# One wq product of each attention layer taken in three f32r passes instead of f32

## The reference

```python
for i in range(12):
    qkv = x @ Wqkv[i].T + bqkv[i]
    q, k, v = jnp.split(qkv, 3, axis=-1)     # 16 heads of 8 channels
    att = jnp.einsum('bhqd,bhkd->bhqk', q, k) * scale
    y = jnp.einsum('bhqk,bhkd->bhqd', att, v)
    x = y @ Wproj[i].T + bproj[i] + x
x = _layernorm(x0 + x)
x = _layernorm(x + ffn(x))
```

## Time and profile before

| | |
|---|---|
| median of 3 executions | 348.29 us (347.01 to 348.66) |
| the profiled execution | 348.11 us, of it 346.3 us span |
| mean granted TensorE clock | 0.995 of full speed |
| TensorE matmul busy | 321.3 us, 93% |
| VectorE busy | 234.9 us, 68% |
| ScalarE (ACT) busy | 184.1 us, 53% |
| GpSimd (POOL) busy | 98.4 us, 28% |

### The profile page before, as it was taken

The page is one execution under the profiler, slowest core; times in us unless marked ns, Lnnn a source line. Parts: engine busy times, 40 slices in busy tenths (PEclk is TensorE's granted clock), DMA queues, the critical chain, the costliest instruction groups (busy, mean ns, idle before and its releaser), DMA issues.

```text
span 346.3 us, 8406 instructions
## 1 busy us (share of the span) xinstructions
PE 321.3 (93%) x3349; PEld 291.2 (84%) x3349; DVE 234.9 (68%) x652; ACT 184.1 (53%) x421; POOL 98.4 (28%) x91
## 2 busy tenths in 40 slices
PE   7596989999999999999999999999999999999994
PEld 7485877979989798897989979799797988888883
DVE  1047888777577575766758767576675568998974
ACT  2142673846748376573855738567383045533350
POOL 2012342305032050410505014050235032654533
PEclk9899999999999999999999999999999999999999
DMA  8910100101001020010100101010000000111112
GB/s 233 403 54 2 60 3 2 59 2 61 2 2 59 3 61 3 2 59 2 61 1 21 41 2 59 2 61 4 2 2 1 2 4 0 30 30 47 46 33 61
DMA packets 10659, 13.65 MB, mean 39 GB/s; under 512 B 512, under 2 KB 8832, under 8 KB 10496
## 3 DMA queue, kind: packets, MB, share of 16 engines
q1 hardware_dynamic: 8224, 11.35, 10.2%
q10 hardware_dynamic: 2400, 1.80, 1.6%
HBM read 11.04 MB, written 2.10 MB: 38 GB/s over the span
## 4 chain that ended last, share of the span: by engine, by line
PE 75%; DVE 11%; DMA 5%; issue 4%; ACT 2%; POOL 1%; ACTq 1%; POOLq 0%; DVEq 0%
PE ps L922 13%; PE ps L963 12%; PE ps L853 12%; PE ps L805 6%; PE ps L803 6%; PE ps L804 6%; DMA xt<-x_tok 5%; PE ps L1042 3%; PE ps L862 3%; PE ps L908 3%; DVE s_rows L636 2%; PE ps L869 2%; DVE xt L738 2%; DVE mt L624 2%; PE ps L1031 1%
## 5 line engine op out<-in xcount | busy, mean ns | idle before, releaser
L371 POOL TENSOR_TENSOR step_lo<-step,step_hi 128x512 fp32r<-128x512 f32 x44 | 54.8, 1275 | 159.6 <-ACT step_hi L461 159.6
L803 PE MATMUL ps<-state_hi,step_hi 128*128 128x258 f32 x176 | 50.7, 288 | 0.0
L922 PE MATMUL ps<-s_rows,w 32*128 32x256 f32 x768 | 44.8, 380 | 5.5 <-DVE s_rows L636 5.5
L805 PE MATMUL ps<-state_hi,step_lo 128*128 128x258 f32 x176 | 49.8, 283 | 0.0
L804 PE MATMUL ps<-state_lo,step_hi 128*128 128x258 f32 x176 | 49.6, 282 | 0.0
L922 PEld LDWEIGHTS ps<-s_rows,w 32*128 32x128 f32 x768 | 40.4, 185 | 7.4 <-ACT s_rows L455 7.4
L963 PE MATMUL ps<-step,gram 128*128 128x128 f32 x352 | 44.7, 281 | 1.2 <-DVE gram L631 1.2
L461 ACT CAST step_hi<-step 128x512 fp32r<-128x512 f32 x44 | 27.0, 619 | 35.4 <-DVE step L641 35.4
L963 PEld LDWEIGHTS ps<-step,gram 128*128 128x128 f32 x352 | 41.0, 192 | 5.4 <-DVE step L641 3.3
L853 PE MATMUL ps<-w,gram 128*128 128x128 f32 x352 | 44.0, 278 | 0.0
L853 PEld LDWEIGHTS ps<-w,gram 128*128 128x128 f32 x352 | 41.1, 192 | 1.0
(11 more groups left out here) (121 smaller groups left out, 512.9 us busy)
## 6 DMA issues: line engine op xcount, KB each, us to landing
w<-weights SPq DMA_DIRECT2D x12, 496.5 KB, 3.5
xchan<-x_chan SPq DMA_DIRECT2D x1, 2048.0 KB, 14.7
out<-xchan SPq DMA_DIRECT2D x7, 256.0 KB, 2.3
xt<-x_tok ACTq DMA_DIRECT2D x4, 256.0 KB, 9.8
xt<-x_tok SPq DMA_DIRECT2D x4, 256.0 KB, 5.7
fw_int<-ffn_weights ACTq DMA_DIRECT2D x1, 576.0 KB, 16.8
out<-xchan SPq DMA_DIRECT2D x2, 128.0 KB, 1.9
cst<-consts ACTq DMA_DIRECT2D x1, 154.5 KB, 4.6
```

The lines of the kernel that those rows point to most:

```text
L371: nc.gpsimd.tensor_tensor(group(step_lo, g), group(step, g), group(step_hi_f, g), ALU.subtract).then_inc(step_lo_ready, 1)
L803: nc.tensor.matmul(dst, l_hi, r_hi, start=True, stop=False)
L805: return nc.tensor.matmul(dst, l_lo, r_hi, start=False, stop=True)
L922: last = nc.tensor.matmul(n_banks(h)[:, k, :], w[r, s, WQ + P * i:WQ + P * (i + 1)], s_rows[r, h, i, :], start=i == 0, stop=i == QUADS - 1)
```

## The change

n_stage(0) stays as it is. For n_stage(1), ACT writes the high part of s (`s_hi`, f32r, two operations of two blocks each) and VectorE the low part (`s_lo`, two operations); wq is split once a layer into `wq_hi` (ACT, at the head of its layer) and `wq_lo` (GpSimd, at the head of its layer). n_stage(1) is then three f32r products for each i. VectorE's sum `mbq` moves behind the first two `add_identity`. SP waits for the split of wq before it loads over the slot.

```diff
+        s_hi = sb("s_hi", [P, QUADS, 2 * P], F32R)
+        s_lo = sb("s_lo", [P, QUADS, 2 * P], F32R)
+        wq_hi = sb("wq_hi", [P, QUADS, P], F32R)
+        wq_lo = sb("wq_lo", [P, QUADS, P], F32R)
 # SP
                 sp.wait_ge(shift_ready, k + 1)
+                sp.wait_ge(wq_split, k + 1)
 # GpSimd, first in the layer
+                pool.wait_ge(wq_hi_set, at(1, 1))
+                nc.gpsimd.tensor_tensor(wq_lo[:, :, :].rearrange("p r c -> p (r c)"), w[:, s, WQ:WQ + QUADS * P],
+                                        wq_hi[:, :, :].rearrange("p r c -> p (r c)").bitcast(F32),
+                                        ALU.subtract).then_inc(wq_split, 1)
 # ACT, first in the layer
+                act.wait_ge(w_in[s], at(8, 16 - 8 * s))
+                if at(1, 0):
+                    act.wait_ge(n_done, at(2, 0))
+                nc.scalar.copy(wq_hi[:, :, :].rearrange("p r c -> p (r c)"), w[:, s, WQ:WQ + QUADS * P]).then_inc(wq_hi_set, 1)
 # ACT, after s
-                for h in range(2):
-                    act.wait_ge(s_done, at(2, h + 1))
-                    nc.scalar.copy(s_rows[:, h, 0:2, :], s_banks(h)[:, 0:2, :]).then_inc(s_low_half_ready, 1)
+                act.wait_ge(s_done, at(2, 1))
+                nc.scalar.copy(s_rows[:, 0:2, :], s_banks(0)[:, 0:2, :]).then_inc(s_low_half_ready, 1)
+                act.wait_ge(s_done, at(2, 2))
+                for i in range(0, QUADS, 2):
+                    nc.scalar.copy(s_hi[:, i:i + 2, :], s_banks(1)[:, i:i + 2, :]).then_inc(s_hi_ready, 1)
 # VectorE
-                take_s(0)
-                take_s(1)
+                take_s()
+                low_of_s(0)
+                low_of_s(2)
...
+                def low_of_s(i):
+                    dve.wait_ge(s_hi_ready, at(2, i // 2 + 1))
+                    nc.vector.tensor_tensor(s_lo[:, i:i + 2, :], s_banks(1)[:, i:i + 2, :], s_hi_f[:, i:i + 2, :],
+                                            ALU.subtract).then_inc(s_lo_ready, 1)
...
-                dve.wait_ge(bqp_ready, at(1, 1))
-                nc.vector.tensor_reduce(mbq[:, :], bqp[:, :, :], AX_X, ALU.add).then_inc(mbq_ready, 1)
                 for h in range(2):
                     add_identity(2 * h)
                     add_identity(2 * h + 1)
+                    if h == 0:
+                        dve.wait_ge(bqp_ready, at(1, 1))
+                        nc.vector.tensor_reduce(mbq[:, :], bqp[:, :, :], AX_X, ALU.add).then_inc(mbq_ready, 1)
 # TensorE, n_stage(h)
+                    else:
+                        pe.wait_ge(s_lo_ready, at(2, 2))
+                        pe.wait_ge(wq_split, at(1, 1))
                     for i in range(QUADS):
+                        f32 = w[:, s, WQ + P * i:WQ + P * (i + 1)]
+                        hi, lo = wq_hi[:, i, :], wq_lo[:, i, :]
+                        parts = ((f32, s_rows),) if h == 0 else ((hi, s_hi), (hi, s_lo), (lo, s_hi))
+                        for p, (left, right) in enumerate(parts):
+                            for k in range(QUADS):
+                                r = slice(QUAD * k, QUAD * (k + 1))
+                                last = nc.tensor.matmul(n_banks(h)[:, k, :], left[r, :], right[r, i, :],
+                                                        start=i == 0 and p == 0, stop=i == QUADS - 1 and p == len(parts) - 1)
```

More of the change, by code:

```diff
@@ L118, in build @@
         step_hi_f = step_hi[:].bitcast(F32)
-        s_rows = sb("s_rows", [P, 2, QUADS, 2 * P])
+        s_rows = sb("s_rows", [P, QUADS, 2 * P])
+        s_hi = sb("s_hi", [P, QUADS, 2 * P], F32R)
+        s_lo = sb("s_lo", [P, QUADS, 2 * P], F32R)
+        s_hi_f = s_hi[:].bitcast(F32)
+        wq_hi = sb("wq_hi", [P, QUADS, P], F32R)
+        wq_lo = sb("wq_lo", [P, QUADS, P], F32R)
         gk = sb("gk", [P, BATCHES, P])
@@ L227, in build @@
         s_high_half_ready = sem("s_high_half_ready")
+        s_hi_ready = sem("s_hi_ready")
+        s_lo_ready = sem("s_lo_ready")
+        wq_hi_set = sem("wq_hi_set")
+        wq_split = sem("wq_split")
         n_done = sem("n_done")
@@ L632, in centre_gram, with take_s @@
                                             ALU.add).then_inc(gram_ready, 2)
-                def take_s(h):
-                    dve.wait_ge(s_done, at(2, h + 1))
-                    nc.vector.tensor_copy(s_rows[:, h, 2:4, :], s_banks(h)[:, 2:4, :]).then_inc(s_high_half_ready, 1)
+                def take_s():
+                    dve.wait_ge(s_done, at(2, 1))
+                    nc.vector.tensor_copy(s_rows[:, 2:4, :], s_banks(0)[:, 2:4, :]).then_inc(s_high_half_ready, 1)
+                def low_of_s(i):
+                    dve.wait_ge(s_hi_ready, at(2, i // 2 + 1))
+                    nc.vector.tensor_tensor(s_lo[:, i:i + 2, :], s_banks(1)[:, i:i + 2, :], s_hi_f[:, i:i + 2, :],
+                                            ALU.subtract).then_inc(s_lo_ready, 1)
                 def add_identity(g):
@@ L914, in n_stage @@
                 def n_stage(h):
-                    pe.wait_ge(s_low_half_ready, at(2, h + 1))
-                    pe.wait_ge(s_high_half_ready, at(2, h + 1))
-                    for i in range(QUADS):
[L920 to L923, removed]
+                    if h == 0:
+                        pe.wait_ge(s_low_half_ready, at(1, 1))
+                        pe.wait_ge(s_high_half_ready, at(1, 1))
+                    else:
+                        pe.wait_ge(s_lo_ready, at(2, 2))
+                        pe.wait_ge(wq_split, at(1, 1))
+                    for i in range(QUADS):
+                        f32 = w[:, s, WQ + P * i:WQ + P * (i + 1)]
[6 more added lines that the diff above has]
+                                                        start=i == 0 and p == 0, stop=i == QUADS - 1 and p == len(parts) - 1)
                     last.then_inc(n_done, 1)
```

## The result

The changed kernel takes 352.67 us (median of 20; before 349.19, also of 20); the ratio of the means is 1.0077, 95% interval 1.0048 to 1.0106. That ratio leaves out the six slow executions of the changed kernel (353.77 us and more), of which the profiled one, 354.89 us, is one; the medians of all are 1.0% apart. The forecast was 345.8 us, faster than before; the changed kernel is slower by 0.8%. Measured again on another chip it was 1.0056 (1.0022 to 1.009).

A forecast was written before the change was run, and what follows sets the result against it. The prediction took TensorE as the bound, with the n products the largest part (13%). It summed 348.11 - 12 x 0.29 (n_stage(1)) + 1.06 (layer 1) + 0.12 (layer 0) = 345.8 us, range 343.8 to 347.8.

The forecast's parts named there:

- n_stage(1): On TensorE, twelve f32r rows at 0.119 us take 1.43 instead of 1.72 us, saving 0.29 us a layer.
- Rival 3: TensorE runs f32r row groups no faster than f32 rows, 0.215 instead of 0.119 us a row: 359.6 us; chance 0.06.
- The tie at the start of n_stage(1): Its s_lo operand and the first half of n are both done at 141.67; booked 0, at worst 0.1 us a layer.
- rival 2: A new wait takes the gain: s_lo late (first part) or kdiag late; 347.0 us, with both 348.2; chance 0.25.
- VectorE behind it: After s_lo, VectorE's mbq and step writes still come in time for H and U; nothing waits.
- wq_hi, wq_lo, kdiag: Head of a layer: the wq split delays vdiag and kdiag, within TensorE's 0.3 us cover; no cost in a steady layer.
- Layer 1: wq_lo queues behind wgu_lo and two xc and blocks VectorE's L595; TensorE waits for mt, + 1.06 us, once.
- the sum: Total of the booked terms: 348.11 - 12 x 0.29 + 1.06 + 0.12 = 345.8 us, starting from the profiled execution.
- Layer 0: vdiag ends at 22.57 instead of 22.45 beside GpSimd's operation, and TensorE waits for VectorE's chain to mt: + 0.12 us.
- The feed-forward part shifts as a whole: Behind the last layer, the feed-forward code only moves in time; nothing booked for it.

The follow-up runs named there:

- the experiment: Changed kernel with the taken feed-forward variant directly behind the branch, mbq's sum put back ahead of the first step: 350.40 us, ratio 1.002.
- both stalls taken away: Changed kernel with the taken feed-forward variant directly behind the branch, GpSimd's wgu_lo and two xc moved to the end of layer 1: 345.57 us, ratio 0.9876.

## Why the prediction was wrong

- *n_stage(1)*: right. A row of four costs 0.12 us, the rate of one f32r matmul on the whole array, and the layer got 0.29 us shorter (21.12 to 20.83), as booked. Rival 3 is out: 48 matmuls in 1.43 us are 30 ns each. That is under half of the 62 ns that the Trainium skill (TensorE: Matmul & The Clock Gate, section "Wait — 56ns, not 53.3ns?") gives for hardware decode off, so its figure doesn't apply to this kernel.
- *The tie at the start of n_stage(1)*: right. s_lo ends 0.05 us ahead of the first product of n_stage(1), TensorE shows no wait, and the layer has its whole 0.29, so rival 2's first part is out.
- *VectorE behind it*: right, and the experiment shows what the order is worth. The prediction had no price for this move; left where it was, mbq's sum would have taken half of the gain.
- *wq_hi, wq_lo, kdiag*: right. vdiag took 0.42 us more (0.45 forecast), kdiag ended 0.5 us ahead of its use.
- *Layer 1*: right in place and kind. L616, which is L595 of before, took 1.58 us instead of 0.56, + 1.02 for the forecast 1.06; TensorE waited 1.00 us for mt, and the layer got 0.58 us longer, which is 0.87 more than its share of the gain. From the start of layer 1 to the start of layer 11 the changed kernel is 2.05 us faster; the terms of the sum for that stretch, 10 x 0.29 - 1.06, give 1.84.
- *Layer 0*: not seen in this profile. The layer's start lay in a half-clock stretch, and vdiag (24.32) came after GpSimd's operation had ended (23.24). In the variants with the branch moved and with both stalls taken away the clock was full there, and vdiag took 0.41 and 0.40 us instead of 0.29, the 0.12 of the sum.
- *"The feed-forward part shifts as a whole"*: this is the step that failed, 5.6 us of it. The prediction booked nothing between the last layer and the end. The sum counted what the new instructions cost the engines and how they wait for one another, not that they move all later code of TensorE. 384 instructions are one and a half blocks of 256, and they moved the branch from a place at which its target had been fetched to one at which it hadn't: 3.07 us. The half clock that goes with the gap took 2.5 more in the profile; why the clock falls there is not shown. Undoing only the move takes both away and brings the time near the forecast. Most of the remaining 1.3 us of the miss is the starting point: the sum began at 348.11 us, the profiled execution, and the median of 20 executions of the kernel before is 349.19.

The Trainium skill (Runtime: NRT & Kernel Launch, section "Instruction fetch mechanics") says that fetching ahead is sequential, in blocks of 16 KiB or 256 instructions, and that a taken branch whose target isn't in the window stalls for a fetch. The trace agrees on the 256 instructions a block, and the experiments on the stall: 0.47 us with the target in it, 3.5 us without, 0.09 us for a branch that falls through. With that rule the jump would have been a rival from the start. Its price, 3.1 us, and the place in a block that misses could not be told from the trace of before: it holds one taken branch over a long stretch of TensorE code, and that one hit. The trace did show that the branch hangs on a block that came only 2.6 us ahead of it.

## What to carry to other kernels

When an edit adds or removes many instructions on an engine whose code is jumped over later, look at that jump as well: in the profile it is an idle time put down to "issue" and a long branch record, a block on the instruction queue within that record is a sign that the code came late, and some harmless instructions at the start (128 here) show in one run whether it is the code's place. Put the variant that is taken directly behind the branch: in the three profiles with that order the branch took 92 ns, at a place where the other order missed (other places were not tried). The jump moves to the end and took 3.4 to 4.0 us there, which is free only where the engine has no more work. A good change can measure as a bad one for this reason alone: here the same edit measures 0.8% slower or 0.7% faster depending on 128 instructions elsewhere.

## What the runs showed of the hardware

- The taken branch of TensorE's sequencer over the unused variant took 465 to 469 ns or 3.5 to 3.8 us by its place. It hit at 0.86 of a block of 256 instructions (23.86, 24.86 and 25.86 blocks ahead of it) and missed at 0.36 (24.36 and 25.36), 0.45 and 0.55. A 16 KB block comes on instruction queue q8 within the branch in each miss and in no hit.
- Four f32r matmuls on four groups of 32 rows run side by side like f32 ones; a row of 256 columns costs 0.12 us where f32 costs 0.216, so three passes of f32r are 1.43 against 1.72 us.
- A VectorE operation with two operands in SBUF ended only after GpSimd's operation beside it: fw 1.58 us instead of 0.56, vdiag 0.71 instead of 0.29. One that starts when two of them are queued can wait for both (kdiag in layer 1, 3.22 us instead of 0.76). One that reads PSUM didn't wait: two `step` writes took 1.29 us from 142.02, with no GpSimd operation, and 1.29 us from 143.74, beside `step_lo` (143.44 to 147.18).
- The gap goes with a stretch at half clock, 3.4 or 6.8 us long in these profiles, that begins near the gap's end. It cost 2.5 us in the profile of the changed kernel, beside 3.1 us of the gap itself.
